# Blocked triangular inverse of a gated delta rule: the upper blocks by VectorE transposes of 32x32 blocks

## The reference, cut to what matters

```
M = where(strictly_lower, (k_b @ k.T) * decay, 0)
Tinv = solve_triangular(eye + M, eye, lower=True)
u = Tinv @ v_b;  w = Tinv @ (k_b * exp(g))
v_new = u - w @ S;  o = qg @ S + attn_loc @ v_new
S = S * exp(g_last) + kdecay.T @ v_new
```

## Time and profile before

| | |
|---|---|
| median of the runs | 1913.42 us |
| the profiled execution, its own time | 1910.49 us |
| its span, first to last instruction | 1908.8 us |
| mean granted TensorE clock | 0.906 |
| busy: TensorE, its weight loads, VectorE, ScalarE, GpSimd | 84%, 60%, 54%, 44%, 26% |

### The profile page before, as it was taken

The page is one execution under the profiler, slowest core; times in us unless marked ns, Lnnn a source line. Parts: engine busy times, 40 slices in busy tenths (PEclk is TensorE's granted clock), DMA queues, the critical chain, the costliest instruction groups (busy, mean ns, idle before and its releaser), DMA issues. The chain is left out here.

```text
span 1908.8 us, 40792 instructions
## 1 busy us (share of the span) xinstructions
PE 1595.2 (84%) x16556; PEld 1148.4 (60%) x16556; DVE 1038.6 (54%) x2155; ACT 846.3 (44%) x1662; POOL 497.1 (26%) x554
## 2 busy tenths in 40 slices
PE   4547888898988889898888889888789967788999
PEld 2235667576766657576665767666565553454765
DVE  5786574646567464655647465664732314464234
ACT  3334545455554545454454545544343304566211
POOL 3451132222313222231323223131313404210100
PEclk9768889898989989898998989998999988799899
DMA  5112010201101020111102010110120020000200
GB/s 181 30 46 81 13 45 17 47 25 26 26 14 43 18 48 25 26 25 15 37 13 59 25 26 24 17 37 13 33 71 12 1 60 2 1 2 1 66 1 22
DMA packets 179610, 60.93 MB, mean 32 GB/s; under 512 B 144832, under 2 KB 172096, under 8 KB 179168
## 3 DMA queue, kind: packets, MB, share of 16 engines
q1 hardware_dynamic: 169216, 50.30, 11.5%
q10 hardware_dynamic: 10208, 8.01, 1.3%
HBM read 39.21 MB, written 19.07 MB: 31 GB/s over the span
## 5 line engine op out<-in xcount | busy, mean ns | idle before, releaser
L1109 POOL TENSOR_TENSOR og<-og,sz 128x256 f32<-128x256 f32 x128 | 93.2, 728 | 711.0 <-DVE og L1051 474.6
L902 DVE SCALAR_TENSOR_TENSOR Yv<-banks,cwall,Yv 128x511 f32<-128x511 f32 (+2 forms) x192 | 131.5, 739 | 53.0 <-ACT Yv L747 53.0
L516 PE MATMUL banks<-wv,xT 128*128 128x512 f32 x256 | 123.6, 628 | 32.2 <-DVE Yv L902 23.1
L656 PE MATMUL banks<-wz,xT 128*128 128x256 f32 x512 | 129.6, 399 | 0.3 <-DVE yacc L1071 0.3
L516 PE MATMUL banks<-wqk,xT 128*128 128x512 f32 x256 | 125.8, 637 | 2.0 <-DVE Yk L902 2.0
L725 PE MATMUL banks<-wo,oT 128*128 128x256 f32 x512 | 124.3, 386 | 0.8 <-ACT oT L894 0.8
L1037 DVE TENSOR_TENSOR St<-Sd,banks 128x256 f32<-128x256 f32 x64 | 26.8, 418 | 162.4 <-PE banks L693 162.0
L656 PEld LDWEIGHTS banks<-wz,xT 128*128 128x128 f32 x512 | 104.0, 206 | 18.4 <-issue 2.3
L1116 POOL TENSOR_TENSOR rn<-ss,c_half 128x4 f32<-128x4 f32 x64 | 64.5, 1008 | 162.6 <-DVE ss L1065 162.6
L516 PEld LDWEIGHTS banks<-wv,xT 128*128 128x128 f32 x256 | 49.3, 201 | 91.3 <-issue 90.9
L725 PEld LDWEIGHTS banks<-wo,oT 128*128 128x128 f32 x512 | 92.5, 190 | 18.5 <-ACT oT L894 6.0
(11 more groups left out here) (356 smaller groups left out, 3792.2 us busy)
## 6 DMA issues: line engine op xcount, KB each, us to landing
cm_d<-CM SPq DMA_DIRECT2D x32, 256.0 KB, 3.9
wqk<-in_L_attn_W_qkvz SPq DMA_DIRECT2D x8, 512.0 KB, 4.6
wv<-in_L_attn_W_qkvz SPq DMA_DIRECT2D x8, 512.0 KB, 4.5
wz<-in_L_attn_W_qkvz SPq DMA_DIRECT2D x16, 256.0 KB, 2.8
wo<-in_L_attn_W_out SPq DMA_DIRECT2D x16, 256.0 KB, 3.1
blk<-cm_d SPq DMA_DIRECT2D x128, 16.0 KB, 1.8
t_d<-tb SPq DMA_DIRECT2D x16, 128.0 KB, 1.7
u_d<-ub SPq DMA_DIRECT2D x16, 128.0 KB, 1.8
```

What stands on the lines that cost most here:

```text
L516: ins = pe.matmul(bank[b][:, :], xT[:, d, b * S + of_batch, :], w[:, d, :], start=(d == 0), stop=(d == KD - 1))
L656: ins = pe.matmul(bank[7][:, b * 256:(b + 1) * 256], xT[:, d, b * S + q, :], wz[:, d, :], start=(d == 0), stop=(d == KD - 1))
L902: v.scalar_tensor_tensor(y, bank[b][:, 0:T - j], conv_w(k, t)[:, 3 - j:4 - j], y, ALU.mult, ALU.add).then_inc(s["tap"].sem, 1)
L1109: pool.tensor_tensor(og[:, n, :, :], og[:, n, :, :], sz[q % 2][:, b, :].rearrange("p (h d) -> p h d", h=VR), ALU.mult).then_inc(s["osz"].s ...
```

## The change

- The blocks of the transposed inverse are no longer brought and multiplied, they are transposed on VectorE in blocks of 32x32: `Ud` from `Td` once after the DMAs (new step `U0`, which waits for them on VectorE), and again after the masked copy (`U16`, now waiting for `T16`). Gone are the pass `U16p` (64 products), the masked copy of `Ud` and its mask `up16`, the copy to `ub`, one of two DMAs to DRAM, 8 of 16 DMAs back and one clearing of a tile on GpSimd.
- `TU32` makes the lower blocks of both halves, 32 products in place of 48; VectorE transposes them from PSUM into `UB` (`U32`), the second one after ScalarE's `T32`.
- Before `TU16` TensorE waits for `U0`; ScalarE's `P32c` no longer waits for `U16p`.
- Another table of times. Sorted as `in_order` does, TensorE's list in heads 1 to 14 becomes: `P16`, `wout0`, `vT0`, `TU16`, `TR3`, `vT1`, `vT2`, `vT3`, `SU3`, `P32`, and further on `TR4`, `pk`, `TU32`, `SU4`; `SU0` stands before `QK`. ScalarE does `vn1` before `V3` (before: `V3`, `vn1`), `vn2` before `Tf`, and `w0` before `V2`. VectorE has `w3` before `og2`, then `U0`, and `U32` before `R5`. SyncE's order stays. In the prologue ScalarE's six casts of weights (`qc`) stand before its copies `xT`, and `k0` before `asp`; VectorE does the first ternary group after `ba`; TensorE turns its first weights after two of the decays.

```diff
@@ AT (some of the changed times)
-    ... "TU16": 50.8, "T16": 52.25, "U16": 52.54, "UBd": 54.13 ...
+    ... "U0": 48.41, "TU16": 50.56, "T16": 52.01, "U16": 52.3, "UBd": 53.35 ...
...
@@ sp_blocks
-        sp.wait_ge(*s["sub"](18, k))
+        sp.wait_ge(*s["sub"](17, k))
         sp.dma_start(t_d, tb[:, 0:256].rearrange("p (i c) -> p i c", c=16)).then_inc(s["tu_out"].sem, 16)
-        sp.dma_start(u_d, ub[:, :, :]).then_inc(s["tu_out"].sem, 16)
-        sp.wait_ge(*s["tu_out"](1, k))
-        sp.wait_ge(*s["TU0"](1, k))
+        sp.wait_ge(*s["tu_out"](0, k))
+        sp.wait_ge(*s["TU0"](0, k))
         for q in range(8):
             rows = slice(q * 16, (q + 1) * 16)
             cols = slice(q % 2 * 16, (q % 2 + 1) * 16)
-            for dst, own in ((Td, t_d), (Ud, u_d)):
-                sp.dma_start(dst[rows, :, cols], own[rows, :, :].rearrange("m i c -> i m c")).then_inc(s["base"].sem, 16)
+            sp.dma_start(Td[rows, :, cols], t_d[rows, :, :].rearrange("m i c -> i m c")).then_inc(s["base"].sem, 16)
@@ pe_inverse
-        pe.wait_ge(*s["base"](15, k))
+        pe.wait_ge(*s["base"](7, k))
...
         pe.wait_ge(*s["P16"](0, k))
+        pe.wait_ge(*s["U0"](0, k))
         pe_blocks(pe, "T16p", b3, lambda g, i: Ud[g, i, :], P2)
-        pe_blocks(pe, "U16p", b2, lambda g, i: P2[g, i, :], Ud)
...
         for i in range(HC):
-            pe.matmul(b2[quarters[1], i * C:(i + 1) * C], Ud[quarters[1], i, :], P2[quarters[1], i, :], start=True, stop=True)
-            for lo, hi in (quarters[0:2], quarters[2:4]):
-                ins = pe.matmul(b2[lo, i * C:(i + 1) * C], P2[hi, i, :], Ud[hi, i, :], start=True, stop=True)
+            for hi in (quarters[1], quarters[3]):
+                ins = pe.matmul(b2[hi, i * C:(i + 1) * C], Ud[hi, i, :], P2[hi, i, :], start=True, stop=True)
@@ act_inverse
-        act.wait_ge(*s["U16p"](0, k))
@@ v_inverse
-        v.tensor_copy(ub[:, :, :], t16.rearrange("p i c -> p c i")).then_inc(s["sub"].sem, 1)
+        yield at(k)["U0"]
+        v.wait_ge(*s["base"](7, k))
+        v.transpose(Ud[:, :, :], Td[:, :, :]).then_inc(s["U0"].sem, 1)
...
         yield at(k)["U16"]
-        v.wait_ge(*s["U16p"](0, k))
-        v.copy_predicated(Ud[:, :, :], rows_of("up16"), chunks(bank[2])).then_inc(s["U16"].sem, 1)
+        v.wait_ge(*s["T16"](0, k))
+        v.transpose(Ud[:, :, :], Td[:, :, :]).then_inc(s["U16"].sem, 1)
...
-        for lo, hi in (quarters[0:2], quarters[2:4]):
-            ins = v.tensor_copy(UB[k % 2][lo, :, hi], chunks(bank[2])[lo, :, :])
+        for lo, hi in (quarters[2:4], quarters[0:2]):
+            if lo == quarters[0]:
+                v.wait_ge(*s["T32"](0, k))
+            ins = v.transpose(UB[k % 2][lo, :, hi], chunks(bank[2])[hi, :, :])
@@ pool_inverse
-        pool.memset(Ud[:, :, :], 0.0).then_inc(s["TU0"].sem, 1)
```

More of the change, by code:

```diff
@@ L147, in constants @@
     c["half"] = con("half", [P, 32])
-    for n in ("up16", "lo16"):
-        c[n] = con(n, [P, C], I32)
+    c["lo16"] = con("lo16", [P, C], I32)
     c["neghalf"], c["poshalf"] = c["half"][:, 0:16], c["half"][:, 16:32]
@@ L200, in on_vector @@
         ch.step(v.tensor_scalar(t[4][:, :], col[:, :], 4, None, ALU.logical_shift_right))
-        for name in ("up16", "lo16"):
-            low, high = (t[4], t[3]) if name == "lo16" else (t[3], t[4])
+        for name in ("lo16",):
+            low, high = t[4], t[3]
             ch.step(v.tensor_scalar(t[5][:, 0:C], low[:, 0:C], 1, None, ALU.bitwise_and))
@@ L331 @@
 FSTEP = 6.53
-GROUPS = (-21.28, 5.52, 19.04, 26.77, 39.04, 48.92, 64.48, 68.98, 72.98, 82.46)
+GROUPS = (-8.9, 5.52, 19.18, 26.77, 39.04, 48.92, 64.48, 68.98, 78.11, 82.68)
 LANES = 2 * S
@@ L346 @@
 FIRST = {
[7 rows of a table removed]
-    "og": 6.71, "Sd": 0.21, "osz": 7.51, "ssq": 0.15, "red": 2.0, "rn": 2.98, "ogn": 6.18, "oTp": 7.01, "oT": 8.32, "wout": 9.14, "y": 12.39, "RECUR": 92.72, "STEP": 8.48, "OUT": 16.51,
[7 rows of a table added]
+    "S": 5.91, "og": 6.71, "Sd": 0.21, "osz": 7.51, "ssq": 0.15, "red": 2.0, "rn": 2.98, "ogn": 6.18, "oTp": 7.01, "oT": 8.32, "wout": 9.14, "y": 12.39, "RECUR": 92.72, "STEP": 8.48,
+    "OUT": 16.51,
 }
@@ L367 @@
 START = {
-    "x": -83.68, "iota": -72.39, "small": -73.36, "const": -75.25, "fill": -35.37, "tb": -68.08, "px": -64.44, "prs": -48.4, "xn": -45, "xTp": -44.19, "xT": -23.46, "pba": -9, "abeta": 0.0,
[3 rows of a table removed]
+    "x": -66.83, "iota": -52.86, "small": -53.83, "const": -55.72, "fill": -10.69, "tb": -73.57, "px": -47.59, "prs": -29.68, "xn": -31.74, "xTp": -33.02, "xT": -18.26, "pba": -9,
+    "abeta": 0.1, "ba": -21.44, "asp": -2.4, "sp1": -1.48, "asp2": -0.37, "sp2": 1.52, "pgs": 3.32, "gc": 4, "pgT": 4.82, "gp": 4.99, "atab": 5.32, "neg": 7.42, "g_d": 10.1, "qin": -56.98,
+    "qin2": -48.45, "qc": -30.87, "qr": 0.32, "qp": 3.32, "qt": 16.1, "qe": 16.24, "r1": -24.91, "q1s": 7.79, "q1t": 60.96, "q1c": 0.32, "q1p": 2.1, "q1tp": 3.49, "q1e": 2.83, "f0in": 72.01,
+    "f0": 66.95, "f0y": 196.81, "fill1": 67.56, "cwp": -28.9, "cwe": -26.59,
 }
@@ L405, in gdn @@
     oT = sb("oT", [P, B, VR, P])
-    cm_d, t_d, u_d = dram("cm_d", [P, HC, 2 * C]), dram("t_d", [P, 16, 16]), dram("u_d", [P, 16, 16])
+    cm_d, t_d = dram("cm_d", [P, HC, 2 * C]), dram("t_d", [P, 16, 16])
     Wq = a["L0_attn_W_qkvz"].rearrange("(k p) (h n) -> p k h n", p=P, n=QKVZ)
@@ L485, in sp_blocks @@
         if k:
-            sp.wait_ge(*s["sub"](18, k - 1))
+            sp.wait_ge(*s["sub"](17, k - 1))
         for q in range(8):
@@ L974, in v_inverse @@
         ch = Chain(v, s["sub"])
-        ch.n = 19 * k
+        ch.n = 18 * k
         for i in range(1, 8):
@@ L981, in v_inverse @@
                 if k:
-                    v.wait_ge(*s["tu_out"](1, k - 1))
+                    v.wait_ge(*s["tu_out"](0, k - 1))
             t3 = t512[:, 0:2 * i * i].rearrange("p (u c j) -> p u c j", u=2, c=i)
@@ L1302, in act_forward @@
             if n == 0:
-                act.wait_ge(*s["sub"](18, LAST))
+                act.wait_ge(*s["sub"](17, LAST))
             elif n == 8:
                 act.wait_ge(*s["P32p"](0, LAST))
+                act.wait_ge(*s["U16"](0, LAST))
             elif n % 8 > 2:
```

6 lines of the change are left out of this document (3 added, 3 removed), and 43 rows, old and new, of tables (AT, FINAL, FIRST, START).

## The result

The kernel after takes 1806.36 us, median of 4 runs (1802.98 to 1810.55); before, beside it, 1910.41 (1906.95 to 1913.73). The ratio is 0.9453, with a 95% interval of 0.942 to 0.9485. The profiled execution took 1810.55 us, with a span of 1808.8. The gain, 99.9 us between the two profiled executions, is larger than the 74.6 that were forecast, and lies outside the range (1815 at its lower end).

What follows compares the result with a forecast made beforehand. TensorE, busy 84% and running one fixed list, was taken to bound the kernel. Gains of 61.6 us (heads 1 to 14), 7 (head 15), 3 (head 0) and 3 (prologue), 74.6 in all, took 1910.5 to 1836; range 1815 to 1874.

Steps and rivals of the forecast that it cites:

- The stretch: TensorE's list from the first pass of P16 to P32: mean 13.5 us to become 9.1, saving 4.4 us a head.
- The subtraction for head 8: From P16 to P32: 12.90 us less 3.69 for the upper pass with its idle time and 1.35 for slow clock.
- The two waits of 0.9 us: Between P16 and P32, TensorE was to idle about 0.5 us before vT3 and 0.4 before SU3, waiting for ScalarE.
- The 0.3 us for what the fetch doesn't cover: Allowance per head for instruction fetch at the packet borders in the first and lower passes.
- The cause of the hole: Issue idle of 2.19 us in head 8's upper pass: TensorE outruns its instruction fetch, so it goes with the pass.
- the rest of a head: Everything in a head outside P16 to P32: 70 to 71.5 us, expected unchanged.
- off the path: VectorE's changes from removed copies against new transposes, at most 0.5 us more a head, were to cost TensorE nothing.
- `TU32`: 64 pairs in place of 96: no gain expected; the other bound was 7 us in all.
- Head 15: Last head's part from P16 to P32, 18.3 us with three holes, was to become 11.3, a gain of 7.
- Head 0 and the prologue: First head to gain 3 us by the pass and its hole; prologue 3, between 0 and 4, by earlier asp.
- the first three: Rivals: hole returns elsewhere, 1878 us (0.14); rest of head grows, 1873 (0.10); transposes contend with GpSimd, slower, 1944 (0.04).
- The fourth: Rival, better: the two new waits and the fetch rest don't show, 1.2 us a head, 1818 us; chance 0.10.

Runs made afterwards that it cites:

- the kernel with the second pass: After, with a second burst of 64 products (the removed upper pass) put back behind the lower pass, its result unread: 1871.78 us, ratio 0.9796.
- the second profiles: The kernels before and after, unchanged, each run once more with a profile: 1906.97 us in one run for before, 1806.86 us for after.
- the turn order: After, with V3 ahead of vn1 on ScalarE and SU3 ahead of vT3 on TensorE in the middle heads, as in before: 1797.39 us, ratio 0.9422.
- two orders back: After, with w0 behind V2 on ScalarE and QK ahead of SU0 on TensorE in the middle heads, as in before: 1815.3 us, ratio 0.9494.
- gate first: After, with z0 alone moved ahead of ssq3 on ScalarE in the middle heads: 1797.91 us, ratio 0.9417.
- all three: After, middle heads: V3 before vn1, SU3 before vT3, z0 ahead of ssq3, S1 and og1 behind taps v3: 1779.09 us, ratio 0.9327.

## Why the prediction was wrong, and where it was right

**The stretch: right.** The subtraction for head 8, 12.90 - 3.69 - 1.35 = 7.86 us, is what the new code shows under the old table (7.86). The two waits of 0.9 us are what the new table adds (0.93; one of them stands in the row of `vT3`, 0.49 us, the other one shows only as small gaps). The 0.3 us for what the fetch doesn't cover are nothing: two idle times, of 0.67 and 0.15 us, in heads 0 to 14. The stretch gave 4.68 us for 4.4, 0.28 x 13 = 3.6 us of the miss.

**The cause of the hole: right, and sharper now.** Instruction fetch it is: moving the border by work elsewhere brings the idle time and takes it away, in the kernel with the second pass it keeps its place, and every such idle time ends 2.2 to 3.0 us behind the start of a packet of instructions. The prediction had "with one pass of 128 between other work a border has 3 us or more", and so "the hole goes with the pass". 3 us are too few: packets start at least 3.2 us apart, and neighbouring borders at which TensorE waits are 3.3 us apart at the least and up to 6.3. In after the two borders of the bursts are about 3.45 us apart by my count, and that just fits. Part of it is the luck of the place, which the prediction had counted rightly, at pair 87 of the first pass, but not priced: 98 pairs of other work ahead of the heads bring the idle time back, 10.4 us of it in the first passes. The Trainium skill (Runtime: NRT & Kernel Launch, Instruction fetch mechanics) calls the crossing mostly hidden; in this case it is where the borders are far enough apart, and costs up to 2.7 us in the bursts of heads 1 to 14 where they are not.

**The step that failed: "the rest of a head".** The prediction left it unchanged, at 70 to 71.5 us, and looked at the new table only for what it might cost. The table cost 0.93 us in the stretch, which was found; it also gave 1.0 us in the rest, which was put at nothing without a reason. The rest fell from 70.64 to 68.96 us, and by the runs these 1.68 us a head come from:

- `SU0` ahead of `QK`: the state copy and first output run on VectorE while TensorE does the scores, so `A` is done 0.33 us earlier for `E0` (the piece is 13.31 us with the old order and 12.98 with the new, on the old code and on the new);
- `w0` ahead of `V2`: the transpose of `og` no longer waits for the gate `sz`, 0.67 us (8.27 and 7.60, again with either code);
- the `ub` copy: 0.28 us. The prediction had VectorE's changes "off the path" in one sentence for all of them. For the transposes that held; the copy lies in the one piece, `E0` to `pw`, that VectorE's taps end last, and there it counts (in head 4 of after, where TensorE runs it at a granted clock of 0.85, it waits 1.32 us for them; in the usual heads it is slower itself, waits less, and the piece is 11.58 us all the same);
- what is left, 0.4 us: pieces longer than usual, most of them at a lower granted clock. The usual lengths add up to 69.86 us in before and 68.58 in after, 1.28 apart; the means are 70.64 and 68.96. In the second profiles the means are 70.89 and 69.17, so this share is much the same; that the change brings it is not shown.

13 x 1.68 = 21.8 us, and with the 3.6 above 25.4 us; 25.3 were missed between the profiled executions, and the errors of the other terms cancel.

**Those other terms.** Head 14 was counted like the others, 4.4, and gave 9.1: its stretch 5.3, the piece behind `P32` 2.7 (15.9 us for 13.2, at a low clock that the second profile of before doesn't have), and the remaining 1.1 the rest. Head 15 gave 4.4 and not 7: an idle time of 3.42 us in its first pass, again in the second profile (3.19) and absent in three kernels with the border at the same place, which the count had not foreseen. Head 0 and the prologue, 3 and 3 forecast, gave 1.1 and 1.3 in the first pair of profiles; over all the profiles with the new table and nothing added ahead of head 0 (10) and with the old one (5) the means are 79.3 and 82.1 us for head 0, 123.1 and 125.6 for the start of its first pass: 2.8 and 2.5 us. These kernels differ in more than the table, and their heads 0 spread over 5 us, so the forecast may have been near, and one pair of profiles is a poor judge.

**The rest of the sum held.** `TU32` brought nothing (13.26 and 13.21 us from `P32` to `P64`, and 13.21 with the third product back). TensorE never waited for `U0`, `U16` or `U32`; the first idle time of line 621 is for ScalarE's `P2`. The transposes were priced at 0.73 and 0.7 us and took 0.705, 0.711 and 0.714. The Trainium skill (Vector Engine (DVE) Microarchitecture Reference, The reshape front-end and per-opcode configuration) has one element per cycle per lane, from which 0.53 us was an estimate without a fixed part; the rows are 0.17 to 0.18 above it.

**The rivals.** None of the first three came. The fourth, better, had the right sign and the wrong place: it sought the surplus in the stretch, where it was 0.3 us, and its 1818 is short of 1806 by the rest of the head. The range ended at 1815 because no term of it let the rest of a head gain. Its own terms, added up at their best, reach 1811 and not 1815 (1836 less 1 for the prologue, 7 for `TU32` and 14 x 1.2 for waits and fetch); the 1806 lies below that too.

**What stays open.** What decides in which heads TensorE's granted clock falls: it differs between two profiles of one kernel, and it took back some 4 us of the turn order's gain and gave some to the kernel with the two orders back. And the idle time of 3.2 to 3.4 us in head 15 is explained in part only. It is instruction fetch again, at a time when the DMA engines are full with other transfers: in after their busy share is 0.95 to 1.04 from 1294 to 1300 us and 0.06 from 1301 on, the packet of instructions starts at 1300.07, and TensorE goes on at 1302.60. The packet before it had started 45 us earlier; in the three kernels without this idle time (two orders back, gate first, all three) one more lies 8 to 20 us ahead of the pass. Why it comes there and not in the others is not known.

## What to carry to other kernels

When a change brings a new table of orders or times along with new code, price it step by step in both directions, and count an edit as off the path only after naming, for the piece in which it lies, the engine that ends it last. Where bursts of very short instructions stand close together, count instructions: an idle time put down to issue that moves by a fixed number of instructions from turn to turn points at the instruction fetch. Adding a few instructions far ahead of the loop tests it: the idle time moves by as many. It goes away by fewer instructions or by longer work between the bursts (6 us did it here, 1 us only by a third). Compare kernels by the usual lengths of the pieces of a repeated turn, which agree to 0.05 us from profile to profile; they show 0.3 us where the total time has a spread of 8. Agreeing sums of pieces prove little: two pieces may have moved against each other.

## What the runs showed of the hardware

- TensorE's instructions come in packets of 16.4 KB, some 128 pairs of short instructions, one at a time: no two start less than 3.2 us apart in 17 profiles, and TensorE goes on 2.2 to 3.0 us after the start of the packet that it waits for, while it goes through 128 pairs in 1.3 us in a burst of 32x32 products. After some 60 us with the packets 8 us and more apart, the second or third border of a rapid series already costs up to 2.7 us.
- The fetch shares the DMA engines: in head 15, with their busy share near 1.0, TensorE waited 3.2 to 3.4 us for it.
- In most heads TensorE is granted the lower of its two levels, 1.2 GHz, behind an idle time of some 2 us (not in head 13 of before, after 2.43 us): four 128x128 products took 1.22 us behind the hole and 0.71 without. So a hole costs more than its length: 1.3 us of burst and 2.1 of hole made the stretch 4.7 us longer.
- A product in a quarter of the array that would be idle was free here: 96 pairs take the time of 64 where the third goes to another quarter (19.9 us for 1024 instructions in line 621 of after, and in line 624 of before, which has it beside the earlier trace rows).
- VectorE's transpose of 32x32 blocks takes the same 0.71 us for 128 partitions by 512 within SBUF and for 32 partitions by 512 out of PSUM.
